# A graph attention layer: steps of 1920 edges at fixed addresses with a carry, in place of one node block per step

## The chip, the core and the metric

The kernel runs on one core of a Trainium2 chip. The metric is the device time of one execution in microseconds (us); lower is better. Five engines work side by side, each through its own instruction stream in order: TensorE (PE; PEld is its weight load), VectorE (DVE), ScalarE (ACT), GpSimd (POOL), and SyncE (SP), which here only issues transfers. They wait for each other on semaphores.

## What is computed

There are 12500 nodes with 64 features, and 212500 edges that are sorted by their target node `dst`. Each edge gets a score, a softmax runs over all edges with the same target, the weighted features of the source nodes are summed, and a dense layer with a residual and a layer norm follows.

```python
h_trans = features @ Watt_w.T + Watt_b
h_src = h_trans[src]
h_dst = h_trans[dst]
e_raw = jnp.sum(h_dst * jnp.tanh(h_src + e_r), axis=-1, keepdims=True)
e_ij = leaky_relu(e_raw * scaling)
max_score = jax.ops.segment_max(e_ij, dst, num_segments=num_nodes)
exp_e = jnp.exp(e_ij - max_score[dst])
denom = jax.ops.segment_sum(exp_e, dst, num_segments=num_nodes)
alpha = exp_e / (denom[dst] + 1e-09)
h_neigh = jax.ops.segment_sum(features[src] * alpha, dst, num_segments=num_nodes)
sum_h = features + h_neigh
prod_h = features * h_neigh
h_out = leaky_relu(sum_h @ W1_w.T + W1_b + (prod_h @ W2_w.T + W2_b))
...
x = _layernorm(x + h_out)
```

## The kernel before

**Head.** TensorE projects all nodes (`project`), VectorE adds the bias and leaves h and x side by side in `hx`; SyncE writes them to `table` in DRAM (L417, L419), one row of 128 numbers for each node. ScalarE and VectorE split all of h into three bf16 parts (`h3`, L629, L1014, L1019). VectorE, TensorE and an indirect transfer find where each block of 128 nodes has its first edge (`find_first`, `set_windows`).

**Steps.** There are 98 blocks of 128 nodes, one a step. A step takes a window of 18 tiles of 128 edges (`MAIN = 17` tiles lie p-major, the `TAIL` tile row by row), starting at the first edge of its block. GpSimd gathers the `table` rows of the sources: one indirect DMA for each tile (L554). The eighteenth tile is gathered only if the block has over 2176 edges; with these inputs the blocks take 1715 gathers. Tiles go in chunks of four (`CHUNK`), so there are five chunks in a step, and three pieces of up to eight tiles.

**The pipeline.** Each engine runs the same function `step(third, before, prev, b, nxt, ahead)`: it works on several blocks at once, b being the newest whose edges are added up, `prev` = b-1, `before` = b-2, `third` = b-3. For b, VectorE adds gathered rows and edge attributes (`add`, L1084), ScalarE takes tanh (L656), TensorE expands h to the edges (`expand`, L819), and VectorE takes the dot products (`dot`, L1095). For `prev` the scores are scanned for their segment maximum: on VectorE across 17 tiles (L1106, L1109), through TensorE into a row (`lay_rows`, L831, L833), two scans along that row (`scan_row`, L1115, L1117), back through TensorE (`lay_back`), and then the exponents' arguments (`exponents`, last line L1128). ScalarE weighs (`weigh`, L681, one activation a tile), TensorE sums (`sum_edges`, L861). For `before` VectorE divides (`neighbours`), TensorE transposes (L867), ScalarE copies (`copy_sum_prod`, L687), TensorE runs the dense layer (`dense`, L872). For `third` VectorE adds the bias, first in its step (L1155), and then the activation, the residual and the moments (`residual`). For `nxt` VectorE builds the one-hot tiles (`place`, `build_hot`, L1073), which TensorE transposes (L805) and ScalarE copies (L651). At a step's end ScalarE prepares the gaps (`set_ids`, L665 to L671) and VectorE writes them (`set_gaps`, L1134, L1135).

**Order and waits.** The order inside a step is that of the calls in each engine's `step`, written by hand. Four steps stand in the body of a hardware loop (`pipeline`: `e.Fori(1, TURNS)`, `BUFS` = 4), so VectorE takes 22 branches back; the first and the last steps are unrolled. GpSimd may gather block b only when the buffer of block b-4 was summed.

**Tail.** The layer norm of all nodes runs after the last step, on GpSimd and VectorE (`normalise`, L369, L371), and SyncE stores four parts of the output (L487, L496).

Of the kernel before, what the change touches and what calls it, by code (L numbers as in the profile page):

```python
# [22 lines left out]
ALU = mybir.AluOpType  # L23
# [7 lines left out]
MAIN = 17  # L31
TAIL = 1
TILES = MAIN + TAIL
# [22 lines left out]
def gnn_layer(nc, x, src, dst, edge_attr, w1, b1, w2, b2, watt, batt, out):  # L56
# [5 lines left out]
    WINDOW = TILES * P  # L62
# [5 lines left out]
    ROW = (2 + TAIL) * P  # L68
    STEPS = [range(a, min(a + STEP, BLOCKS)) for a in range(0, BLOCKS, STEP)]
    ROW_STEP, FIRST_STEP, WINDOW_STEP = 0, 11, 12  # L70
    LAG = 13
    PIECE = STEP * (len(STEPS) // PIECES)
    TURNS = (BLOCKS - 2) // BUFS
# [9 lines left out]
    assert D == 64 and ROWS * SEARCH_ROW == E and TURNS * BUFS + 2 == BLOCKS and BLOCKS % 2 == 0  # L83
    assert (BLOCKS - (PIECES - 1) * PIECE) * D <= MAIN * (2 * D + 1) and BUFS == PIECES
    assert BLOCKS + 1 <= P and ROWS <= P and WINDOW <= E and LAST_NODES > 0

    with ExitStack() as ctx:  # L87
# [13 lines left out]
        def by_piece(name):  # L101
# [11 lines left out]
        h3 = sb("h3", [P, BLOCKS, 3, D], BF16)  # L113
# [17 lines left out]
        bound_i = sb("bound_i", [P, 1], I32)  # L131
        bound = sb("bound", [P, 1])
        bound_row_i = sb("bound_row_i", [P, P], I32)
        bound_row = sb("bound_row", [P, P])
        row_last = sb("row_last", [P, 1])
        below_row = sb("below_row", [P, P])
        row_f = sb("row_f", [P, 1])
        row_idx = sb("row_idx", [P, 1], I32)
        below_n = sb("below_n", [P, 1])
        first = sb("first", [P, 1])  # L140
        first_row = sb("first_row", [1, P + 1])
        next_first = sb("next_first", [P, 1], I32)
        falls = sb("falls", [P, 1])
        row_falls = sb("row_falls", [P, 1])
        over_row = sb("over_row", [1, P])
# [3 lines left out]
        start_row = sb("start_row", [1, P])  # L149
        count_row = sb("count_row", [1, P])  # L150
        start_i = sb("start_i", [1, P], I32)
        count_i = sb("count_i", [1, P], I32)
# [7 lines left out]
        row_i = [sb(f"row_i{k}", [1, ROW], I32) for k in range(2)]  # L160
# [7 lines left out]
        here = sb("here", [P, MAIN])  # L168
        away = sb("away", [P, MAIN])
        gap = sb("gap", [P, MAIN + 1])  # L170
        from_first = sb("from_first", [P, MAIN])
        from_last = sb("from_last", [P, MAIN])
        row_here = sb("row_here", [1, ROW])
        row_gap = sb("row_gap", [1, ROW + 1])
        row_max = sb("row_max", [1, ROW])
        run_max = sb("run_max", [P, MAIN])
        part_max = sb("part_max", [P, MAIN])
        first_max = sb("first_max", [P, MAIN])
        edge_max = sb("edge_max", [P, MAIN])
# [12 lines left out]
        mean_var = sb("mean_var", [P, 2])  # L192

        spare = weight[:, :, :].rearrange("p g n -> p (g n)")
        rows_i = spare[:, 0:SEARCH_ROW].bitcast(I32)
        below = hotT[1][:, :, :].rearrange("p g n -> p (g n)")[:, 0:SEARCH_ROW]
# [3 lines left out]

        hrest = [[hot[2 + j][:, 8 * k:8 * (k + 1), :].rearrange("p g n -> p (g n)").bitcast(F32) for k in range(2)]
                 for j in range(2)]
# [21 lines left out]
        ps_hd = [bank(f"ps_hd{k}") for k in range(3)]  # L224
        ps_hot = [bank(f"ps_hot{k}", BF16) for k in range(2)]
# [3 lines left out]
        ps_sc = [ps_hd[2], ps_row]  # L229
        a_sum = ps_acc[:, 0:D + 1]  # L230
        a_out = ps_acc[:, 256:256 + D]
        row_iota = ps_row[:, ROW:ROW + P // 2].bitcast(BF16)
        numbers = hot[0][:, 0, :]
        m_back = ps_misc[:, 0:2 + TAIL]
        m_spT = ps_misc[:, 128:256]

# [18 lines left out]
        rows_counted = sem("rows_counted")  # L255
        row_ps = sem("row_ps")
        row_ready = sem("row_ready")
        rows_got = sem("rows_got")
        first_ready = sem("first_ready")
        first_ps = sem("first_ps")  # L260
        first_sb = sem("first_sb")
# [5 lines left out]
        part_done = [sem(f"part_done{k}") for k in range(3)]  # L267
# [1045 lines left out]
```

## Time and profile before

| what | value |
|---|---|
| median of 3 runs | 2266.44 us (2265.88 to 2267.22) |
| profiled execution | 2264.81 us, its span 2263.1 us |
| POOL busy | 1655.6 us (73%), x1739 |
| PE busy | 1479.7 us (65%) |
| DVE busy | 1273.0 us (56%) |
| ACT busy | 1085.1 us (48%) |
| granted TensorE clock | 0.5 of 2.4 GHz in the steps |
| moved by DMA | 188.03 MB, 83 GB/s in the mean |

The profiled execution lies 1.6 us under the median. Busy shares are means over the span. A group of instructions is written as line, engine, operation, output<-inputs; after the bar stand the busy time, the mean of one in ns, and the idle time of the engine before them. In the order of time, a row begins with the start and the duration in us, and ends, in brackets, with the idle time of the engine before it and what ended it. "issue" stands for idle time in which the engine waited for nothing that the profile shows.

### The profile page before, as it was taken

What the parts mean: (1) busy time and instruction counts of PE and PEld (TensorE: products, weight loads), DVE (VectorE), ACT (ScalarE), POOL (GpSimd) and SP (SyncE); (2) the same over time, 40 slices, a digit from 0 to 9 for tenths busy, and PEclk for the clock granted to TensorE, in tenths of its full rate; (3) what the DMA queues carried; (4) which work ended last, traced back from release to release, by engine and by line L of the source; (5) the groups of instructions that cost most, each with busy time, mean ns of one, the idle gap of its engine ahead of it and who ended that gap; (6) DMA issues with size and microseconds to landing.
All of it is one profiled execution on the core that took longest, in us unless ns stands there. A gap on an engine that the chain in (4) does not pass through costs nothing.

```text
span 2263.1 us, 43202 instructions
## 1 busy us (share of the span) xinstructions
PE 1479.7 (65%) x11621; PEld 1370.9 (61%) x11621; DVE 1273.0 (56%) x7138; ACT 1085.1 (48%) x3198; POOL 1655.6 (73%) x1739
## 2 busy tenths in 40 slices
PE   3466767667676666676676776766766666766762
PEld 3365656566665666566565665656656665665662
DVE  5556555546556555565555565564655656555554
ACT  3454445545454454545454454544545544454552
POOL 1777777777777777777777777777777777777773
PEclk8555555555555555555555555555555555555555
DMA  8333233232323333232333323333332323323322
GB/s 201 95 76 86 75 86 84 75 85 74 85 75 84 77 83 85 75 85 75 85 82 77 85 74 86 80 79 79 80 86 74 85 77 82 85 74 85 82 67 57
DMA packets 205576, 188.03 MB, mean 83 GB/s; under 512 B 152630, under 2 KB 165228, under 8 KB 205436
## 3 DMA queue, kind: packets, MB, share of 16 engines
q0 software_dynamic: 55040, 113.18, 19.3%
q1 hardware_dynamic: 150396, 73.62, 13.0%
q14 instruction: 129, 1.06, 0.2%
q8 instruction: 11, 0.18, 0.0%
HBM read 177.04 MB, written 9.60 MB: 82 GB/s over the span
## 4 chain that ended last, share of the span: by engine, by line
POOL 64%; issue 24%; POOLq 5%; PE 3%; DVE 1%; DMA 1%; SPq 1%; ACT 1%; DVEq 0%; ACTq 0%
POOL got L554 63%; PE ps_acc L861 2%; POOLq L564 2%; POOLq L544 2%; SPq L417 1%; DMA weight<-in_dst 1%; ACT weight L681 1%; POOL hx L369 0%; DMA got<-table,src_i 0%; POOLq L561 0%; POOLq L87 0%; POOL hx L371 0%; DVE hot L1073 0%; PE ps_hd L758 0%; PE ps_row L769 0%
## 5 line engine op out<-in xcount | busy, mean ns | idle before, releaser
L554 POOL DMA_INDIRECT got<-table,src_i x1715 | 1625.6, 948 | 549.9 <-issue 549.0
L861 PE MATMUL ps_acc<-got,weight 128*128 128x65 f32 x3528 | 805.4, 416 | 253.9 <-ACT weight L681 205.7
L861 PEld LDWEIGHTS ps_acc<-got,weight 128*128 128x128 f32 x3528 | 781.8, 332 | 277.4 <-issue 200.7
L681 ACT ACTIVATE weight<-hot,arg 128x128 f32<-128x128 bf16 x1764 | 544.5, 389 | 44.4 <-DVE arg L1128 44.4
L656 ACT ACTIVATE edge<-edge 128x256 f32<-128x256 f32 (+1 forms) x490 | 190.3, 389 | 761.1 <-DVE edge L1084 749.4
L1095 DVE CUSTOM_DVE_ANT_0 edge<-edge,ps_hd 128x64 f32<-128x64 f32 x1764 | 288.3, 216 | 422.7 <-issue 392.5
L651 ACT ACTIVATE hotT<-ps_hot 128x1024 bf16<-128x1024 bf16 (+1 forms) x294 | 235.8, 803 | 279.9 <-PE ps_hot L805 272.3
L1084 DVE TENSOR_TENSOR edge<-edge,got 128x256 f32<-128x256 f32 (+1 forms) x490 | 196.2, 400 | 249.0 <-DMA got<-table,src_i 240.9
L819 PEld LDWEIGHTS ps_hd<-h,hotT 128*128 128x128 bf16 x5292 | 324.5, 135 | 15.1 <-issue 0.6
L805 PE MATMUL ps_hot<-ident,hot 128*128 128x128 bf16 x1764 | 242.4, 309 | 132.5 <-DVE hot L1073 128.9
L819 PE MATMUL ps_hd<-h,hotT 128*128 (+1 forms) x5292 | 321.1, 242 | 0.4 <-DVE raw L1095 0.4
L805 PEld LDWEIGHTS ps_hot<-ident,hot 128*128 128x128 bf16 x1764 | 185.3, 146 | 166.5 <-DVE hot L1073 162.1
L831 PE MATMUL ps_row<-ident,part_max 128*1 128x128 f32 x196 | 57.4, 396 | 196.0 <-DVE part_max L1109 129.9
L1073 DVE TENSOR_TENSOR hot<-ps_row,dst_rel 128x512 bf16<-128x512 bf16 (+1 forms) x490 | 167.0, 391 | 9.3 <-DVE base L1065 6.7
L1095 DVE DVE_READ_ACCUMULATOR2_ANT raw<- 128x1 f32 x1764 | 144.7, 82 | 2.6 <-issue 2.6
L831 PEld LDWEIGHTS ps_row<-ident,part_max 128*1 128x1 f32 x196 | 10.6, 80 | 209.4 <-issue 209.4
L845 PE MATMUL ps_misc<-ident,row_max 1*128 1x1 f32 x196 | 36.1, 251 | 121.1 <-issue 117.6
L845 PEld LDWEIGHTS ps_misc<-ident,row_max 1*128 1x128 f32 x196 | 30.6, 203 | 134.2 <-issue 134.2
L1117 DVE TENSOR_TENSOR_SCAN row_max<-row_gap,ps_row 1x384 f32<-1x384 f32 x98 | 92.3, 941 | 3.3
L1115 DVE TENSOR_TENSOR_SCAN ps_row<-row_gap,ps_row 1x384 f32<-1x384 f32 x98 | 92.4, 943 | 0.5 <-PE ps_row L833 0.5
L1155 DVE TENSOR_TENSOR z<-ps_acc,b 128x64 f32<-128x64 f32 x98 | 22.0, 225 | 121.2 <-issue 106.7
L872 PE MATMUL ps_acc<-w12T,sum_prodT 128*128 128x64 f32 x196 | 61.8, 419 | 0.4 <-ACT sum_prodT L687 0.4
(120 smaller groups left out, 1059.7 us busy)
## 6 DMA issues: line engine op xcount, KB each, us to landing
edge<-in_edge_attr SPq DMA_DIRECT2D x98, 544.0 KB
got<-table,src_i POOLq DMA_INDIRECT x1715, 2.5
table<-hx SPq DMA_DIRECT2D x12, 512.0 KB
edge<-in_edge_attr SPq DMA_DIRECT2D x98, 32.0 KB
got<-in_x SPq DMA_DIRECT2D x3, 768.0 KB, 14.5
src_i<-in_src SPq DMA_DIRECT2D x98, 8.5 KB
src_i<-in_src SPq DMA_DIRECT2D x98, 0.5 KB
dst_i<-in_dst SPq DMA_DIRECT2D x98, 8.5 KB
```

Of the source, the lines that this page charges most:

```text
L554: pool.indirect_dma_start(got[b.four][:, g, 0:2 * D], None, table, bass.IndirectOffsetOnAxis(ap=src_i[b.four][:, g:g + 1], axis=0))\
L651: act.activation(hotT[b.two][:, a:z, :], ps, ACT.Copy, bias=1.0, scale=-1.0).then_inc(hot_sb[p], 1)
L656: act.activation(edge[b.two][:, a:z, :], edge[b.two][:, a:z, :], ACT.Tanh).then_inc(tanh_done[c], 1)
L681: last = act.activation(weight[:, g, :], hot[b.four][:, g, :], ACT.Exp, bias=arg[:, g:g + 1], scale=-MASKED)
L805: last = pe.transpose(ps_hot[(b.two + p) % 2][:, k * P:(k + 1) * P], hot[b.four][:, g, :], ident16[:, :])
L819: last = pe.matmul(expanded(g), hotT[b.two][:, g, :], rhs, start=(part == 0), stop=(part == 2))
L861: last = pe.matmul(a_sum, weight[:, g, :], got[b.four][:, g, D:2 * D + 1], start=(g == 0), stop=(g == TILES - 1))
L1073: dve.tensor_tensor(hot[b.four][:, a:z, :].rearrange("p g (n a) -> p g n a", a=2), row_iota.rearrange("p (z n a) -> p z n a", z=1, a=2).to ...
L1084: dve.tensor_tensor(edge[b.two][:, a:z, :], edge[b.two][:, a:z, :], got[b.four][:, a:z, 0:D], ALU.add).then_inc(added[c], 1)
L1095: last = dve.tensor_tensor_reduce(out=edge[b.two][:, g, :], in0=edge[b.two][:, g, :], in1=expanded(g), scale=1.0, scalar=0.0, op0=ALU.mult ...
L1115: chain("row", dve.tensor_tensor_scan(ps_row[0:1, 0:ROW], row_gap[:, 0:ROW], ps_row[0:1, 0:ROW], LOWEST, ALU.add, ALU.max), b)
L1117: dve.tensor_tensor_scan(row_max[:, ROW - 1::-1], row_gap[:, ROW:0:-1], ps_row[0:1, ROW - 1::-1], LOWEST, ALU.add, ALU.max).then_inc(row_d ...
```

## The change

A step takes 15 tiles, which are 1920 edges at a fixed address (step n begins at edge 1920 n), whatever nodes they belong to; the last step ends with the last edge. That makes 111 steps (`WINDOWS`) and 1665 gathers. `TAIL` and the conditional gather are gone, and so are the search for first edges and the splitting of h in the head. A step has four chunks and two pieces. The block of 128 nodes of a step begins at the target of its first edge (`base_all`).

A node may have edges in two steps. So the row scan starts from the last value of the step before (`carried`), and the partial sums of the last node go on: `take_carry` on TensorE picks a row of `sums` with `sel`, `copy_carry` on ScalarE brings it to SBUF, and `sum_edges` adds it with `carry_weight`.

What was done for all nodes in the head or the tail is now done in each step: SyncE loads the step's h and x (`load_h`, `load_nodes`), ScalarE and VectorE split h (`split_h`), ScalarE takes a square root (`deviation`), VectorE normalises (`normalise_nodes`), SyncE stores 128 rows (`store_nodes`). VectorE's addition of the dense layer's bias stays first in its step (`add_bias`). `TURNS` becomes 27, with four steps in the loop's body as before.

```diff
-MAIN = 17
-TAIL = 1
-TILES = MAIN + TAIL
+TILES = 15
...
-    TURNS = (BLOCKS - 2) // BUFS
+    TURNS = (FINAL - 2) // BUFS
...
+            def split_h(b, part):
+
+                if part == 0:
+                    act.wait_ge(h_in[b.two], (b.twos + 1) * 16)
+                    if follows(b, 2):
+
+                        act.wait_ge(hd_ready[NP - 1], b.n - 1)
+                    act.activation(h3[b.two][:, 0, :], hw[b.two][:, :], ACT.Copy, scale=SCALE).then_inc(h_high, 1)
+                else:
+                    act.wait_ge(h_left_set, b.n + 1)
+                    act.activation(h3[b.two][:, 1, :], h_left[:, :], ACT.Copy).then_inc(h_mid, 1)
...
+            def deviation(b):
+                act.wait_ge(own["aggr"], b.n + 1)
+                act.activation(std1[:, :], mean_var[:, 1:2], ACT.Sqrt, bias=eps_col[:, 0:1]).then_inc(std_set, 1)
+
+            def copy_carry(b):
+                act.wait_ge(carry_ps, b.n + 1)
+                act.activation(carry_row[:, :], m_carry, ACT.Copy).then_inc(carry_sb, 1)
...
                 if exists(prev):
                     weigh(prev, 1)
+                if exists(before):
+                    copy_sum_prod(before)
+                if exists(prev) and carried(prev):
+                    copy_carry(before)
+                if exists(third):
+                    deviation(third)
                 if exists(b):
                     tanh(b, 3)
-                if exists(before):
-                    copy_sum_prod(before)
-                if exists(prev):
-                    weigh(prev, 2)
-                if exists(nxt):
-                    copy_hot(nxt, 2)
-                if exists(b):
-                    tanh(b, 4)
                     set_ids(b)
...
+            def take_carry(b):
+                pe.wait_ge(own["sum"], b.n + 1)
+                pe.matmul(m_carry, sel[b.four][:, :], sums[:, :], start=True, stop=True).then_inc(carry_ps, 1)
...
+                    if g == TILES - 1 and carried(b):
+
+                        pe.wait_ge(consts, 5)
+                        pe.wait_ge(carry_sb, b.n)
+                        pe.matmul(a_sum[0:1, :], carry_weight[:, :], carry_row[:, :], start=False, stop=False)
...
             def step(third, before, prev, b, nxt, ahead):
                 if exists(third):
-                    residual(third, 0)
+                    add_bias(third)
                 if exists(prev):
                     finish_scores(prev)
                 if exists(third):
-                    residual(third, 1)
+                    finish_nodes(third)
...
                 if exists(prev):
                     exponents(prev)
+                if exists(nxt):
+                    split_h(nxt, 0)
                 if exists(b):
                     add(b, 2)
                     dot(b, 1)
...
                     add(b, 3)
                     dot(b, 2)
-                    add(b, 4)
+                if exists(third):
+                    normalise_nodes(third)
+                if exists(b):
                     dot(b, 3)
-                    dot(b, 4)
                     set_gaps(b)
```

How the instructions stand on ScalarE, in the loop's body, from the second group of weights of a step to the last tanh of the step. Before:

```order
L681 ACTIVATE weight<-hot,arg 128x128 x8
L656 ACTIVATE edge<-edge 128x256
L687 ACTIVATE sum_prodT<-ps_misc 128x128
L681 ACTIVATE weight<-hot,arg 128x128 x2
L651 ACTIVATE hotT<-ps_hot 128x256
L656 ACTIVATE edge<-edge 128x128
L665 ACTIVATE here<-dst_i 128x17
```

The same place of the changed kernel:

```order
L721 ACTIVATE weight<-hot,arg 128x128 x7
L727 ACTIVATE sum_prodT<-ps_misc 128x128
L735 ACTIVATE carry_row<-ps_spare 1x65
L731 ACT_TABLE_LOAD
L731 ACTIVATE std<-mean_var,eps_col 128x1
L691 ACT_TABLE_LOAD
L691 ACTIVATE edge<-edge 128x192
L695 ISA
L700 ACTIVATE here<-dst_i 128x15
```

The tanh of the fourth chunk now stands behind the copies of the products and of the carry and behind a square root with a table load on each side of it; the third group of weights and the third copy of one-hot tiles are gone.

On TensorE, in the loop's body, from the transposes of the one-hot tiles to the dense layer. Before:

```order
L805 MATMUL ps_hot<-ident,hot 128x128 x16
L861 MATMUL ps_acc<-got,weight 128x65 x8
L867 MATMUL ps_misc<-ident,sum_prod 128x128
L861 MATMUL ps_acc<-got,weight 128x65 x8
L805 MATMUL ps_hot<-ident,hot 128x128 x2
L861 MATMUL ps_acc<-got,weight 128x65 x2
L872 MATMUL ps_acc<-w12T,sum_prodT 128x64
```

The same place of the changed kernel:

```order
L842 MATMUL ps_hot<-ident,hot 128x128 x15
L900 MATMUL ps_acc<-got,weight 128x65 x8
L910 MATMUL ps_misc<-ident,sum_prod 128x128
L906 MATMUL ps_spare<-sums,sel 1x65
L900 MATMUL ps_acc<-got,weight 128x65 x6
L899 MATMUL ps_acc<-carry_row,carry_weight 1x65
L900 MATMUL ps_acc<-got,weight 128x65
L915 MATMUL ps_acc<-w12T,sum_prodT 128x64
```

The summing is 15 tiles in two groups where it was 18 in three, and two products for the carry stand among them.

## Rows read from the trace of the kernel before

**Rows 1.** The page: its span, and the group of the gathers.
```profile
span 2263.1 us, 43202 instructions
L554 POOL DMA_INDIRECT got<-table,src_i x1715 | 1625.6, 948 | 549.9 <-issue 549.0
```
**Rows 2.** Busy times by stretch, 300 to 2100 us; then first and last gather (timeline).
```profile
300.00:2100.00 1800.00, 1217.50 (x9580) 1128.24 (x9580) 1020.23 (x5896) 878.33 (x2620) 1362.17 (x1437) 0.50 0.31 81
...
57.22 0.99 POOL L554 DMA_INDIRECT got<-table,src_i  x1 [27.49 <-issue]
...
2204.26 0.94 POOL L554 DMA_INDIRECT got<-table,src_i  x1 [0.30 <-issue]
```
**Rows 3.** Timeline of VectorE over one step of the loop, 1319.95 to 1340.53 us.
```profile
1319.95 0.23 DVE L1155 TENSOR_TENSOR z<-ps_acc,b 128x64 f32<-128x64 f32 x1
...
1327.81 0.17 DVE L1128 TENSOR_TENSOR arg<-score,edge_max 128x17 f32<-128x17 f32 x1
...
1334.44 0.22 DVE L1095 CUSTOM_DVE_ANT_0 edge<-edge,ps_hd 128x64 f32<-128x64 f32 x1 [2.36 <-issue]
...
1338.73 0.22 DVE L1095 CUSTOM_DVE_ANT_0 edge<-edge,ps_hd 128x64 f32<-128x64 f32 x1 [3.64 <-issue]
...
1339.80 0.23 DVE L1134 TENSOR_TENSOR gap<-here 128x16 f32<-128x16 f32 x1 [0.70 <-ACT row_here L671]
...
1340.53 0.23 DVE L1155 TENSOR_TENSOR z<-ps_acc,b 128x64 f32<-128x64 f32 x1
```
**Rows 4.** Timeline of ScalarE and TensorE over the same step.
```profile
1328.02 2.44 ACT L681 ACTIVATE weight<-hot,arg 128x128 f32<-128x128 bf16 x8 [0.35 <-DVE arg L1128]
...
1330.60 3.65 PE L861 MATMUL ps_acc<-got,weight 128*128 128x65 f32 x16 [2.43 <-ACT weight L681]
...
1334.05 0.42 PE L867 MATMUL ps_misc<-ident,sum_prod 128*128 128x128 f32 x1
...
1334.50 0.28 ACT L687 ACTIVATE sum_prodT<-ps_misc 128x128 f32<-128x128 f32 x1 [0.19 <-PE ps_misc L867]
...
1338.30 0.30 ACT L656 ACTIVATE edge<-edge 128x128 f32<-128x128 f32 x1
...
1338.63 0.63 PE L872 MATMUL ps_acc<-w12T,sum_prodT 128*128 128x64 f32 x2
```
**Rows 5.** A turn of four steps by stretch; VectorE where the loop begins anew; waits.
```profile
1386.30:1473.30 87.00, 59.53 (x468) 55.20 (x468) 49.71 (x289) 42.89 (x128) 65.97 (x70) 0.50 0.32 81
...
1299.01 0.23 DVE L1155 TENSOR_TENSOR z<-ps_acc,b 128x64 f32<-128x64 f32 x1 [4.61 <-issue]
...
DVE z L1155 <- issue: 106.7, 22, 5.6
```
**Rows 6.** Timeline of ScalarE around the first square root.
```profile
2208.65 1.28 ACT L693 ACT_TABLE_LOAD   x1
2209.94 0.38 ACT L693 ACTIVATE std<-stats,eps_col 128x93 f32<-128x93 f32 x1
2210.34 1.28 ACT L681 ACT_TABLE_LOAD   x1
```
**Rows 7.** Groups of VectorE's scans and one-hot builds, by form.
```profile
L1117 DVE TENSOR_TENSOR_SCAN row_max<-row_gap,ps_row 1x384 f32<-1x384 f32 x98 | 92.3, 941 | 3.3
...
L1106 DVE TENSOR_TENSOR_SCAN run_max<-gap,score 128x17 f32<-128x17 f32 x98 | 19.2, 196 | 3.3
...
L1073 DVE TENSOR_TENSOR hot<-ps_row,dst_rel 128x512 bf16<-128x512 bf16 x392 | 147.6, 418 | 9.3 <-DVE base L1065 6.7
...
L1073 DVE TENSOR_TENSOR hot<-ps_row,dst_rel 128x256 bf16<-128x256 bf16 x98 | 27.6, 281 | 0.0
```
**Rows 8.** Timeline of VectorE: the bias addition at the first block and in the drain.
```profile
127.55 0.22 DVE L1155 TENSOR_TENSOR z<-ps_acc,b 128x64 f32<-128x64 f32 x1
...
2209.33 0.23 DVE L1155 TENSOR_TENSOR z<-ps_acc,b 128x64 f32<-128x64 f32 x1
...
2225.57 0.23 DVE L1155 TENSOR_TENSOR z<-ps_acc,b 128x64 f32<-128x64 f32 x1 [9.90 <-PE ps_acc L872]
```

More of the change, by code:

```diff
@@ L334, in pipeline, with carried, edge_at @@
                     turn(t, k)
[L335 removed]
+            for k in range(TURNS * BUFS, WINDOWS + 3):
                 turn(0, k)
         def exists(b):
[L339 removed]
+            return not b.known or 0 <= b.n < WINDOWS
+        def carried(b):
+            return not b.known or 0 < b.n < FINAL
+        def edge_at(b):
+            return E - W if b.known and b.n == FINAL else b.n * W
         def follows(b, n):
@@ L411, in _, with load_indices @@
                     .then_inc(bias_in, 16)
+            def load_indices(b):
+                o = edge_at(b)
+                for tile, vector in ((src_i[b.four], src), (dst_i[b.four], dst)):
+                    sp.dma_start(tile[:, :], vector[bass.ds(o, W)].rearrange("(p g) -> p g", g=TILES))\
+                        .then_inc(index_in[b.four], 16)
+            for n in range(2):
+                load_indices(at_block(0, n))
+            sp.wait_ge(old_set, 1)
+            sp.dma_start(out[N - P:N, :], y_old[:, :]).then_inc(stored, 16)
             for s, blocks in enumerate(STEPS):
@@ new lines, in load_nodes, with store_nodes @@
+            def load_nodes(b, n):
+                sp.dma_start(xw[b.four][:, :], x[bass.ds(n, P), :]).then_inc(xw_in[b.four], 16)
+            def store_nodes(b, n):
+                sp.wait_ge(stored, 16 * (b.n + 1))
+                sp.wait_ge(y_done, b.n + 1)
+                sp.dma_start(out[bass.ds(n, P), :], y_out[b.two][:, :]).then_inc(stored, 16)
+                if b.known and b.n == FINAL - 1:
+                    sp.wait_ge(stored, 16 * (FINAL + 1))
+                    sp.dma_start(y_old[:, :], out[N - P:N, :]).then_inc(old_in, 16)
@@ L679, in weigh @@
                     act.wait_ge(summed[p], b.n)
+                if p == 0 and carried(b):
+                    if follows(b, 2):
+                        act.wait_ge(summed[NP - 1], b.n)
+                    act.activation(carry_weight[:, :], carry_arg[:, :], ACT.Exp)
                 for g in range(*piece(p)):
@@ L844, in lay_back @@
                 for k in range(2):
-                    pe.transpose(m_back[:, k:k + 1], row_max[0:1, k:2 * P:2], ident[0:1, 0:1])
-                for k in range(TAIL):
-                    last = pe.transpose(m_back[:, 2 + k:3 + k], row_max[0:1, (2 + k) * P:(3 + k) * P], ident[0:1, 0:1])
+                    last = pe.transpose(m_back[:, k:k + 1], row_max[b.two][0:1, k:ROW:2], ident[0:1, 0:1])
                 last.then_inc(back_ps, 1)
@@ L1206, in step @@
                 if exists(before):
-                    neighbours(before)
+                    dve.wait_ge(xw_in[before.four], (before.fours + 1) * 16)
+                    neighbours(before, xw[before.four][:, :])
+                if exists(nxt):
+                    split_h(nxt, 1)
                 if exists(b):
```

589 lines of the change are left out of this document (294 added, 295 removed).

## The prediction

> **What bounds the kernel now.** I read the page first, then busy times by stretch, then the steps in the order of time. By the page GpSimd looks like the bound: 1715 gathers, each 948 ns busy with some 0.3 us of issue around it [rows 1]. Between 300 and 2100 us it makes 1437 gathers, one in 1.2526 us, and never pauses between the first at 57.2 and the last at 2204.3 us [rows 2]. A block with 17 or 18 gathers (17.5 in the mean) thus takes 21.9 us, four take 87.7 us. If that were all, 1665 gathers in place of 1715 would save 63 us, and the work taken out of the tail some 30 more.
>
> The timeline of a single step says otherwise. From one bias addition to the next VectorE takes 20.58 us [rows 3], and in this step it waits for no gather; its waits are 2.36 and 3.64 us before dot products (for tanh on ScalarE) and 0.70 us for the gaps. A whole turn of the loop without such a wait takes 87.0 us [rows 5], against 87.7 us for its gathers. So two chains run at nearly the same pace: the gathers, and a circle through VectorE, ScalarE and TensorE. The change lightens the first one. What matters is the second, and it has to be read link by link.
>
> **The circle before.** Count from A, the start of the last argument instruction at 1327.81. From the bias addition to A are 7.86 us of VectorE [rows 3]. From A: ScalarE starts the weights at A+0.21 and TensorE the sums at A+2.79; the transpose of the products follows 3.45 us later (eight tiles), ScalarE copies it at A+6.69; the summing of the rest, the third group of one-hot tiles and the last tanh follow, at A+10.49; VectorE's next bias addition comes 2.23 us after that tanh, at A+12.72 [rows 3, 4].
>
> **The circle after, first half.** The two scans along the row shrink from 384 to 256 elements. The slope from 17 to 384 elements is (941-196)/367 = 2.0 ns, so each saves 0.26 us, together 0.52 [rows 7]. The last two one-hot builds of a step, 512 and 256 wide (418 and 281 ns), become one of 384, about 350 ns: 0.35 less, or 0.27 as such instructions overlap by some 0.08. The copy of the moments goes (0.1 on the path); the carry's argument takes the place of the tail's, and the base is a copy from a table: +0.05. 7.86-0.52-0.27-0.10+0.05 = 7.02 us.
>
> **Second half.** ScalarE has an exponential of one element for the carry before the weights: +0.10 (nearest rows say 0.1 to 0.3). The sums start at A+2.89, the transpose at A+6.34, its copy at A+6.79. TensorE runs at its lower clock of 1.2 GHz, 0.50 granted, throughout [rows 5], and I keep that. The carry's product takes two TensorE passes of 0.22 us each (3.45 us for sixteen) behind the transpose, so ScalarE copies the carry at A+7.15 and is done at A+7.4. Now comes the square root. Exp and tanh share a table in the steps before, where no load is seen; the square root is the one function that brings loads. From the start of one load to the start of the next are 1.69 us with a square root of 93 columns [rows 6], 1.61 with one column; with the second load of 1.28 these are 2.9 us, in every step, ahead of the tanh of the last chunk. This tanh starts at A+10.3, at the same place as before, though three tiles of work are gone. From it to the next bias addition are 2.23 us, +0.05 for 192 instead of 128 columns, -0.25 for shorter row instructions: A+12.34. The splitting of h, `normalise_nodes` and the shorter weights lie in waits: VectorE's 2.36 and 3.64 us before dot products shrink but don't vanish. If that cover were gone, they would cost their 0.2 us each, some 1 us.
>
> So a straight step takes 7.02+12.34 = 19.36 us, 1.22 us less than before, with three tiles less. Fifteen gathers take 18.8 us. The gathers are no longer the bound; GpSimd will wait for free buffers.
>
> **A rule against the trace.** Around the first square root the load begins 0.02 us behind the instruction before it, and the square root 0.01 us after the load's end [rows 6]. The Trainium skill, ScalarE: Activation LUTs, What ACT_TABLE_LOAD costs, gives 1283 ns for the load, as here, and about 1380 ns of drain on top. The trace here shows no such drain. By that figure a step would be longer by 2.8 us and the kernel, as an estimate, by some 300 us. I go by the rows and keep the rule as a rival. The same page says to batch functions of one set; the change does the reverse of that, which fits the 2.9 us above.
>
> **Branches back.** Where the loop begins anew, VectorE sits idle 4.61 us before its bias addition although TensorE has long delivered; there are 22 such waits, 106.7 us in all, as many as branches back [rows 5]. The body still has four steps, so I keep this: a turn of 87.0 us becomes 87.0 - 4 x 1.22 = 82.1 us. There are 26 turns now, for 104 steps.
>
> **The sum.** The first bias addition for a real block came at 127.55 us [rows 8], 52 gathers and 5.2 us after the first gather at 57.2 [rows 2]. The head loses the search but gains six small transfers ahead of the table's, so I leave the first gather at 57 us; with 45 gathers the addition comes at 119 us. Then 108 steps to the drain: 26 x 82.1 + 4 x 19.4 - 4.7 (the last turn has no branch back; 87.0 - 4 x 20.58 = 4.7) = 2207 us, so the drain starts at 2326 us, where before it started at 2209.3 us. The drain's first step took 16.2 us [rows 8] and becomes 15; the last two blocks, a square root each, and a store, a read of the stored rows and a last store one behind the other, about 15 more. The layer norm and the large stores of the tail are gone. 2326+30 = 2356 us of span. With 1.7 us around it, as in the profiled execution of before, that is 2358 us, against 2264.8 us: 4.1% slower. As that execution lies 1.6 us under the median, the comparison with the median is the same within 0.1%.
>
> In short: from the first bias addition to the drain, 95 steps in 2082 us become 108 steps in 2207 us, +125 us; the first addition comes 8.5 us earlier, and from the drain's start to the end there are 30 us in place of 53.8, which gives back 24.
>
> **Bounds.** Each 0.1 us in a step is 11 us. The unknown small instructions (exponential and copies of the carry, three more on ScalarE's queue, waits with registers) leave a step between 18.9 and 19.9 us: 2308 to 2416 us. A branch back of nothing to 7 us: -118 to +55 us. Head and drain: 10 us either way.
>
> **Rivals.** *TensorE's half becomes the last link.* The bias addition waits for `dense`, which stands behind the sums with their two carry products. I get its end at A+11.3, 1 us before VectorE asks. Should the carry cost TensorE over 1 us more, VectorE waits at the start of each step; 0.5 us beyond that point costs 54 us: about 2412 us. For it: two waits between engines stand in the middle of the sums. Against it: TensorE's share falls from 18 to 15 tiles. 0.13.
>
> *The drain exists.* 2.8 us a step, 300 us: about 2660 us. 0.03, as the rows show none.
>
> *The square root is off the path (faster).* If tanh came early enough in spite of it, TensorE's half would decide, A+11.3: 1.0 us a step less, 2250 us, 0.7% faster. It decides as soon as under 1.9 us of the 2.9 are left on the path. Against it: the instruction order leaves ScalarE no choice. 0.05.
>
> *The branch back gets cheap (faster).* Without these 4.7 us the time would be 2358 - 25 x 4.7 = 2240 us, 1.1% faster; the sign turns where under 1 us of them is left. Against it: all 22 branches of before show it, and the body is only some 7% shorter. 0.07.
>
> *The gathers stay the bound (faster).* Both chains shorter than I think: 57+1665 x 1.2526 = 2143, +36 for the last chunk and the drain = 2180 us, 3.8% faster. It needs steps of 18.8 us with the branch in them, 1.7 us less than I count. 0.04.
>
> **The numbers.** The forecast, 2358 us, has 0.68. Its own range is 2300 to 2420. For 8 in 10 I take 2290 to 2435 us: the three faster cases (0.16) stay outside, TensorE's is inside. A measurement tells 0.2% from no change. Faster by over 0.2% are these three, 0.16; within 0.2% I leave 0.02, taken from the forecast's low end; slower is the rest, 0.82.
>
> **What would show it.** In the trace of the changed kernel: two table loads a step, 2.9 us between the carry's copy and the tanh of three tiles; VectorE idle before the dot products of the last chunk; straight steps of 19.4 us and turns of 82 us; GpSimd waiting for the sums of TensorE (before, 0.9 us in all [rows 1]), over 5% of the span; the drain after 2320 us. Wrong it is if VectorE waits for gathers in most steps, if its wait for ScalarE's last tanh is absent, or if it waits for `dense` in every step and not once a turn.

## The result: 2.4% faster, where 4.1% slower was forecast

The changed kernel takes 2212.27 us (median of 4, 2211.41 to 2212.53), the kernel before 2266.58 us (median of 4, 2265.88 to 2267.22). The ratio is 0.9759, with a 95% interval of 0.9747 to 0.9770. The forecast was 2358 us, its range began at 2290. The profiled execution took 2212.15 us, with a span of 2210.4 us, so the sum of the prediction (a span of 2356 us) is 146 us too high.

### The profile page after: what moved, and what is told of

Same layout as the page of the kernel before. It is cut to its first block, busy times and chain, and to the rows that moved or that the text cites. A ratio compares the mean times of both kernels' runs of the same rounds, so it can differ in the third digit from the quotient of the medians.

```text
span 2210.4 us, 44930 instructions
## 1 busy us (share of the span) xinstructions
PE 1523.2 (69%) x11357; PEld 1326.2 (60%) x11357; DVE 1259.5 (57%) x7377; ACT 1401.7 (63%) x3892; POOL 1594.2 (72%) x1678
## 4 chain that ended last, share of the span: by engine, by line
ACT 32%; DVE 30%; PE 21%; issue 11%; POOL 2%; SPq 2%; DVEq 1%; DMA 0%; ACTq 0%; POOLq 0%
PE ps_acc L900 18%; ACT weight L721 11%; ACT L691 6%; ACT L731 6%; DVE hot L1097 5%; DVE edge L1108 4%; DVE ps_row L1140 3%; DVE edge L1119 3%; POOL got L595 2%; DVE row_gap L1163 2%; ACT edge L691 2%; PE ps_spare L906 2%; ACT row_here L706 2%; ACT std L731 1%; DVE edge_max L1150 1%
## 5 line engine op out<-in xcount | busy, mean ns | idle before, releaser
L595 POOL DMA_INDIRECT got<-table,src_i x1665 | 1587.2, 953 | 539.9 <-issue 506.9
L900 PEld LDWEIGHTS ps_acc<-got,weight 128*128 128x128 f32 x3330 | 735.4, 329 | 359.5 <-issue 342.9
L721 ACT ACTIVATE weight<-hot,arg 128x128 f32<-128x128 bf16 x1665 | 506.3, 384 | 5.3 <-DVE arg L1156 5.3
L1119 DVE CUSTOM_DVE_ANT_0 edge<-edge,ps_hd 128x64 f32<-128x64 f32 x1665 | 267.6, 213 | 124.7 <-ACT edge L691 122.8
L857 PE MATMUL ps_hd<-h,hotT 128*128 128x64 bf16 x4995 | 311.1, 242 | 10.5 <-DVE h L1088 10.5
L842 PE MATMUL ps_hot<-ident,hot 128*128 128x128 bf16 x1665 | 213.1, 306 | 148.9 <-DVE hot L1097 148.9
L1203 DVE RECIPROCAL rstd<-std 128x1 f32<-128x1 f32 x111 | 18.2, 164 | 497.4 <-ACT std L731 497.4
L842 PEld LDWEIGHTS ps_hot<-ident,hot 128*128 128x128 bf16 x1665 | 155.8, 138 | 186.2 <-DVE hot L1097 186.2
L674 ACT ACTIVATE hotT<-ps_hot 128x1024 bf16<-128x1024 bf16 x222 | 212.3, 956 | 19.0 <-PE ps_hot L842 17.7
L691 ACT ACT_TABLE_LOAD x108 | 138.6, 1283 | 1.9
L727 ACT ACTIVATE sum_prodT<-ps_misc 128x128 f32<-128x128 f32 x111 | 30.8, 277 | 85.0 <-PE ps_misc L910 85.0
L1140 DVE TENSOR_TENSOR_SCAN ps_row<-row_gap,row_max,ps_row 1x256 f32<-1x256 f32 x109 | 80.2, 736 | 0.0
```

Of the source, the lines that this page charges most:

```text
L595: pool.indirect_dma_start(got[b.four][:, g, 0:2 * D], None, table, bass.IndirectOffsetOnAxis(ap=src_i[b.four][:, g:g + 1], axis=0))\
L674: act.activation(hotT[b.two][:, a:z, :], ps, ACT.Copy, bias=1.0, scale=-1.0).then_inc(hot_sb[p], 1)
L691: act.activation(edge[b.two][:, a:z, :], edge[b.two][:, a:z, :], ACT.Tanh).then_inc(tanh_done[c], 1)
L721: last = act.activation(weight[:, g, :], hot[b.four][:, g, :], ACT.Exp, bias=arg[:, g:g + 1], scale=-MASKED)
L842: last = pe.transpose(ps_hot[p][:, k * P:(k + 1) * P], hot[b.four][:, g, :], ident16[:, :])
L857: last = pe.matmul(expanded(g), hotT[b.two][:, g, :], h3[b.two][:, part, :], start=(part == 0), stop=(part == 2))
```

## The profile after, beside that of before

The page of the changed kernel: its span, the gathers, the queue that brings instructions, and the chain that ended last (share of the span by engine).

```profile
span 2210.4 us, 44930 instructions
...
q14 instruction: 18, 0.15, 0.0%
...
ACT 32%; DVE 30%; PE 21%; issue 11%; POOL 2%; SPq 2%; DVEq 1%; DMA 0%; ACTq 0%; POOLq 0%
...
L595 POOL DMA_INDIRECT got<-table,src_i x1665 | 1587.2, 953 | 539.9 <-issue 506.9
```

The chain no longer runs through GpSimd: it is ScalarE, VectorE and TensorE that hand each other the work. So the gathers ceased to be the bound, as forecast. The page of before has this row for the same queue of instructions:

```profile
q14 instruction: 129, 1.06, 0.2%
```

That is 111 packets of instructions more than after. The prediction does not use this row.

One straight step on VectorE, ScalarE and TensorE (timeline: start, duration, engine and line, idle time before in brackets). It answers to [rows 3, 4]. It is the shortest of its turn: by position behind the branch, the four steps take 19.40, 19.29, 18.92 and 19.07 us in the mean of 25 turns.

```profile
1000.38 0.23 DVE L1186 TENSOR_TENSOR z<-ps_acc,b 128x64 f32<-128x64 f32 x1
...
1003.96 0.24 DVE L1071 TENSOR_SCALAR dst_rel<-dst_i,base 128x30 bf16<-128x30 int32 x1
...
1007.08 0.16 DVE L1156 TENSOR_TENSOR arg<-score,edge_max 128x15 f32<-128x15 f32 x1
...
1009.95 3.65 PE L900 MATMUL ps_acc<-got,weight 128*128 128x65 f32 x16 [2.48 <-ACT weight L721]
...
1014.16 0.22 ACT L735 ACTIVATE carry_row<-ps_spare 1x65 f32<-1x65 f32 x1
1014.39 1.28 ACT L731 ACT_TABLE_LOAD   x1
1015.68 0.29 ACT L731 ACTIVATE std<-mean_var,eps_col 128x1 f32<-128x1 f32 x1
1016.00 1.28 ACT L691 ACT_TABLE_LOAD   x1
...
1017.29 0.36 ACT L691 ACTIVATE edge<-edge 128x192 f32<-128x192 f32 x1
...
1017.59 0.63 PE L915 MATMUL ps_acc<-w12T,sum_prodT 128*128 128x64 f32 x2
...
1019.27 0.23 DVE L1186 TENSOR_TENSOR z<-ps_acc,b 128x64 f32<-128x64 f32 x1
```

Counted from A, the start of the argument instruction at 1007.08: the first half took 6.70 us (forecast 7.02), the carry's copy stands at A+7.08 (7.15), the last tanh at A+10.21 (10.3), TensorE's dense ends at A+11.1 (11.3), the second half took 12.19 us (12.34). Between the carry's copy and the last tanh stand the two table loads with the square root.

VectorE's waits over the whole span (total, times, longest):

```profile
DVE rstd L1203 <- ACT std L731: 497.4, 111, 7.2
...
DVE edge L1119 <- ACT edge L691: 122.8, 108, 1.3
...
DVE z L1186 <- DVE row_gap L1163: 13.1, 27, 0.5
```

VectorE waits 4.5 us a step for the square root (497.4 / 111) and 1.1 us for the last tanh. At the branch back there are 0.5 us in all, where before there were 4.85 us in the mean (106.7 / 22) [rows 5]. A turn of four steps took 76.65 us; 82.1 were forecast:

```profile
1000.38:1077.03 76.65, 54.32 (x408) 47.18 (x406) 44.73 (x264) 50.48 (x140) 58.07 (x61) 0.50 0.32 84
```

The first bias addition and those of the drain:

```profile
117.74 0.23 DVE L1186 TENSOR_TENSOR z<-ps_acc,b 128x64 f32<-128x64 f32 x1 [2.12 <-PE ps_acc L915]
...
2186.17 0.23 DVE L1186 TENSOR_TENSOR z<-ps_acc,b 128x64 f32<-128x64 f32 x1
2200.33 0.23 DVE L1186 TENSOR_TENSOR z<-ps_acc,b 128x64 f32<-128x64 f32 x1 [0.88 <-PE ps_acc L915]
2204.57 0.23 DVE L1186 TENSOR_TENSOR z<-ps_acc,b 128x64 f32<-128x64 f32 x1
```

So the 146 us are: the first addition 1.3 us earlier than forecast; 108 steps in 2068.4 us (2186.17 - 117.74) in place of 2207, 138.6 us; the drain 24.2 us in place of 30, 5.8 us. The step with the branch back takes 0.3 us more than the others (19.40 beside 19.09 us in the mean), where 4.7 were forecast. So of the 138.6 us, 25 x 4.4 = 110 are the branches back; the other 29 are 0.27 us a step.

## Experiments

The question is why the stall at the branch back is gone, and what it would have cost. Theory A: it is a matter of place. VectorE's instructions are fetched in packets, few are held (kept in the engine), and whether the loop's body is still held at the branch depends on where its ends lie between the edges of the packets. Theory B: of size, the body being short enough now. Theory C: the stall had another cause, outside VectorE's stream.

In the built programs, counted with waits and register instructions, VectorE's loop body has 356 instructions at 557 to 913 before, and 341 at 491 to 832 after. (The first expectations count without waits.)

To move the body and nothing else, K tiny instructions are put ahead of the loop, inside a wait of 15.5 us that VectorE has there for its first rows:

```
             dve.memset(ones[:, :], 1.0)
+            for k in range(K):
+                dve.memset(filler[:, k:k + 1], 1.0)
```

### First set: 70, 140, and 60 in the kernel before

> The changed kernel with 70 tiny instructions more on VectorE (one column each, into a tile that nobody reads) ahead of the first step, inside a wait of 16 us for the first rows. Nothing in the loop changes; only the place of the loop's body in VectorE's instruction stream does, from about 424 to 713 (counted without waits) to about 494 to 783. Theory A (place): the branch back costs its 4 to 5 us when the body of VectorE's loop lies over two multiples of 256 instructions (before: 472 to 787, over 512 and 768) and nothing when it lies over one (after: 424 to 713, over 512 alone). It expects 25 waits of about 4.7 us ahead of the bias addition, 2212 + 25 x 4.7 = about 2330 us, and about as many packets in the queue of instructions as before had (129, against 18 of after). Theory B (size): the body is short enough at 289 instructions and was too long at 315, wherever it lies: 2212 us and 18 packets, no change. Theory C (other engines, or the gathers): what vanished was never VectorE's own; 2212 us, no change. The Trainium skill, Runtime: NRT & Kernel Launch, Instruction fetch mechanics, says that instructions come in blocks of 256, that an engine holds two of them, and that a taken branch out of these two has to fetch its target first; theory A is this rule applied to VectorE.

> The changed kernel with 140 such instructions ahead of the first step: the loop's body stands at about 564 to 853, over 768 alone. Theory A (place) expects no wait at the branch back and 2212 us within 0.3%, although the stream is longer than in the run with 70. If any growth of the stream brought the stall back, it would be here as well, about 2330 us. Theories B and C: 2212 us.

> The kernel before with 60 such instructions ahead of the first step: its loop's body of 315 instructions moves from about 472 to 787 to about 532 to 847, over 768 alone. Theory A (place): the 22 waits of 4.6 to 4.9 us go, and the packets of the instruction queue fall from 129 to under 30; the time hardly moves (2255 to 2267 us, 0 to 0.5% less), since the gathers, at 1.2526 us each and never pausing, set 87.7 us for a turn whose circle took 87.0 with the stall. What VectorE no longer waits for at the branch it then waits for at gathered rows. Theory B (size): the stall stays in place, 2266 us, 129 packets. If the gathers did not set the pace of before, the time would fall by the stall, 22 x 4.7 = 103 us, to about 2165 us.

The chip of these runs took 3864 us for the kernel before, so of this set only places and counts of packets are used. The packets of instructions were 143 with 70, 144 with 140, and 129 in the kernel before with 60. (The times were 3224, 3210 and 3859 us.) The first fits theory A and speaks against B and C: the same body of 341 instructions is fetched anew in every turn. The second and the third contradict theory A as I had put it, with blocks of 256.

The records of the single packets gave the right sizes. Each carries 8192 bytes. In a turn of before there are five: two behind the branch back, and three when VectorE has started about 586, 718 and 841 instructions of its program; in the run with 140 the places are about 719, 836 and 971. So an edge comes about every 128 instructions, at about the same places of the program in both. That one is fetched ahead and four are held is inferred: a body that touches three packets would stay held, one that touches four would lose its first. Then 70 (561 to 902), 140 (631 to 972) and 60 in before (617 to 973) all touch four.

### Second set: 20, 110, 43 in the kernel before

> The changed kernel with 20 tiny instructions more on VectorE ahead of the first step. The records of the earlier runs give theory A (place) its right numbers: the instructions of VectorE come in packets of 8 KB, one each 128 instructions; in before five packets come in every turn of the loop, two of them behind the branch back, the others when VectorE is about 586, 714 and 842 instructions into its program (counted with waits and registers), so edges lie at 74 + 128 k. Four packets are held, and one more is fetched ahead, so a body that touches three packets stays held and one that touches four has to be fetched anew at each branch back. Body of before: 557 to 913, four packets (edges 586, 714, 842). Of after: 491 to 832, three (586, 714). With 20 more it is 511 to 852, over the edge at 842 too: four. Theory A expects the wait at the branch back to return (25 x 4.3 to 5 us): 2320 to 2335 us, and 135 to 150 packets in the queue of instructions. Theory B (size alone, 341 instructions against 356) expects 2212 us and 18 packets. The runs with 70 and 140 had over 140 packets, which speaks against B already, but not in a time that can be set beside the 2212 us.

> The changed kernel with 110 such instructions: the body lies at 601 to 942, over the edges at 714 and 842 alone: three packets. Theory A (place): no wait at the branch back, under 25 packets in the queue of instructions, 2212 us within 0.3%. A theory by which every lengthening of the head brings the stall back, in the way that the runs with 70 and 140 did: 2325 us and over 130 packets.

> The kernel before with 43 such instructions: its body of 356 moves from 557 to 913 to 600 to 956, over the edges at 714 and 842 alone: three packets. Theory A: the 22 waits of 4.6 to 4.9 us ahead of the bias addition go, and so do over 100 packets of instructions. The time hardly moves, as the gathers (1.2526 us each, 87.7 us a turn) pace this kernel: 2252 to 2267 us, 0 to 0.6% less. Theory B (the longer body is too long wherever it lies): 129 packets, 2266 us, the waits where they were. If the circle and not the gathers had set the pace of before: 22 x 4.7 = 103 us less, 2163 us.

Measured, on a chip with before at 2270.57 us:

| run | body | time, us | ratio to before | packets |
|---|---|---|---|---|
| 20 more | 511 to 852 | 2275.87 | 1.0023 (1.0013 to 1.0032) | 143 |
| 110 more | 601 to 942 | 2212.51 | 0.9746 (0.9729 to 0.9762) | 19 |
| before, 43 more | 600 to 956 | 2269.01 | 0.9994 (0.9985 to 1.0004) | 19 |

The bodies of 110 and 43 have the same row of packets on their pages:

```profile
q14 instruction: 19, 0.16, 0.0%
```

With 20, the queue of instructions on the page, and VectorE's waits ahead of the bias addition:

```profile
q14 instruction: 143, 1.17, 0.2%
```
```profile
DVE z L1189 <- issue: 77.8, 25, 3.4
```

The same waits with 110:

```profile
DVE z L1189 <- DVE row_gap L1166: 13.4, 27, 0.6
```

In the kernel before with 43, these and the waits for gathered rows:

```profile
DVE edge L1087 <- DMA got<-table,src_i: 620.9, 404, 4.1
...
DVE z L1158 <- DVE row_gap L1138: 11.5, 23, 0.6
```

And the waits for gathered rows in the kernel before as it was:

```profile
DVE edge L1084 <- DMA got<-table,src_i: 240.9, 164, 3.9
```

Theory A holds in both kernels and both ways. 20 instructions bring the stall to the changed kernel, 110 do not; 43 take it from the kernel before, although its body is no shorter. Size alone (B) and another cause (C) are out. In the kernel before the time did not follow: what VectorE no longer waited at the branch it waited for gathered rows, 620.9 us in place of 240.9. The circle with its stall was hidden by the gathers there.

One number missed: with 20 I expected 2320 to 2335 us. The stall is back in all 25 places but costs 63 us (2275.87 - 2212.51), 2.5 us each: it is 3.1 us long here (77.8 / 25, with the usual 0.5 us in it), 4.85 in before (106.7 / 22, [rows 5]).

### Where the edge lies

> The changed kernel with 8 tiny instructions more on VectorE ahead of the first step: the loop's body lies at 499 to 840, its end just short of the edge at 842. Theory A (place, edges at 74 + 128 k) expects no wait at the branch back, under 25 packets in the queue of instructions and 2212 us within 0.2%; 12 instructions more, as in the run with 20, gave 143 packets and 2276 us. If the edge lies lower than I read it, or if the few instructions between the last step and the branch count twice, the stall is here already: 2276 us and over 140 packets.

2278.98 us beside 2274.14 of before, ratio 1.0021 (1.0012 to 1.0031), 143 packets. VectorE's waits ahead of the bias addition:

```profile
DVE z L1189 <- issue: 80.3, 25, 3.5
```

My reading of the edge was too high by a few instructions. A likely reason is that the count goes by instructions that had started, and the fetch runs ahead of them. A body that ends at 832 is held, one that ends at 840 is not, so the edge lies between, and the others 128 apart. All nine bodies agree with this. The changed kernel escapes the stall by at most 8 instructions; 8 more in front of it cost 2.7% (1.0021 beside 0.9759). Neither the shorter body nor its earlier start would have done alone, by this rule: 341 instructions from 557 end at 898, 356 from 491 end at 847, both over the edge. That sum wasn't run.

The Trainium skill, Runtime: NRT & Kernel Launch, Instruction fetch mechanics, says that a taken branch out of the pages held forces a fetch of its target before execution goes on; the traces agree (a fetch in every turn, and VectorE idle until it has come). It gives blocks of 256 instructions and two of them held. By that a body would stall where it has two edges inside, 256 apart. The stalls at 557 to 913 and at 511 to 852 then need an edge between 557 and 596, and the stall at 631 to 972 needs one between 631 and 716: no place of the edges gives both. The traces show packets of 128, and the measurement decides.

### Why the stall was longer in the kernel before

From VectorE's branch in the records, in us: the start of the packet with the branch's target, the first packet of the bulk load of edge features (544 KB before, 480 KB after), and the bias addition.

| kernel | target packet | bulk load | bias addition |
|---|---|---|---|
| before | 2.0 to 3.3 | 0.3 to 0.9 | 4.2 to 5.5 |
| changed, 20 more | 1.0 to 1.3 | 1.9 to 2.0 | 2.9 to 3.2 |
| before, bulk load later | 1.0 to 1.3 | 2.5 to 2.9 | 2.9 to 3.3 |

Busy times by stretch in the kernel before around one such branch (at 1030.2; the bias addition follows at 1034.98). The last three columns are TensorE's clock, the busy share of the DMA engines and GB/s.

```profile
1031.00:1032.00 1.00, 0.00 (x0) 0.00 (x0) 0.00 (x0) 0.00 (x0) 0.70 (x2) 0.50 0.49 164
1032.00:1033.00 1.00, 0.00 (x0) 0.00 (x0) 0.00 (x0) 0.00 (x0) 0.69 (x2) 0.50 1.03 418
1033.00:1034.00 1.00, 0.00 (x0) 0.00 (x0) 0.00 (x0) 0.00 (x0) 0.72 (x1) 0.50 0.82 173
```

The packets of instructions and the bulk load both go through the DMA engines, and for a microsecond these are busy throughout, while VectorE, TensorE and ScalarE stand still. The experiment issues the bulk load some 2 us later, in the kernel before:

```
-                sp.dma_start(edge[b.two][:, 0:MAIN, :], ...)
-                sp.dma_start(edge[b.two][:, MAIN:TILES, :], ...)
+                for q in range(0, P, P // 4):
+                    sp.dma_start(edge[b.two][q:q + P // 4, MAIN:TILES, :], ...)
+                sp.dma_start(edge[b.two][:, 0:MAIN, :], ...)
```

> The kernel before, stall and all, with one thing changed on SyncE: the small load of the last tile's edge features (32 KB) goes ahead of the large one (544 KB), and in four pieces, so that the large load is issued some 2 us later. It is about the size of the stall: 4.6 us in before, where the first packet of the large load starts 0.35 to 0.75 us behind VectorE's branch and the packet of instructions that the branch asks for only 2.0 to 3.2 us behind it; 2.9 us in the run with 20, where the large load starts 1.9 us behind the branch and the instructions come at 1.0 us. If the instructions queue behind the large load in the DMA engines, they come at 1.0 us here too, and the waits ahead of the bias addition at the branch fall from 4.2 to 5.5 us to 2.9 to 3.2 us. If the difference is of another kind (the longer body, the place of the target), the waits stay over 4.2 us. The time stays near 2268 us in either case (the gathers pace this kernel), or rises if the edges come too late.

The same waits here:

```profile
DVE z L1156 <- issue: 70.0, 22, 3.4
```

All 22 waits fell, from 4.85 us in the mean to 3.18 (70.0 / 22). So the bulk load had held the instructions up, most likely as they queued behind it. The time was 2278.19 us, ratio 1.0017 (1.0007 to 1.0026): again the gathers hid what was saved, and VectorE waited 429.2 us for gathered rows in place of 240.9.

### The square root off the path

On ScalarE, the square root is moved from ahead of the last tanh to behind the first:

```
                 if exists(b):
                     tanh(b, 0)
+                if exists(third):
+                    deviation(third)
+                if exists(b):
                     tanh(b, 1)
...
-                if exists(third):
-                    deviation(third)
                 if exists(b):
                     tanh(b, 3)
```

> The changed kernel with the square root (and so its two table loads, 2.9 us with it) taken from between the tanh of the third chunk and the tanh of the last one to between the first and the second tanh of the step, where VectorE has delivered its variance as well. If the loads on the path set the step (19.07 to 19.4 us straight, as forecast), the last tanh comes up to 2.9 us earlier, and TensorE's dense end at A+11.1 us (11.1 + 6.7 = 17.8 us, with the bias addition behind it about 18.2) or the gathers (15 x 1.2526 = 18.8 us) become the bound: 104 to 108 steps at 18.8 us in place of 19.16 us, 2170 to 2185 us. If the loads delay the middle tanhs by as much as they save, no change: 2212 us. If they delay the middle ones and VectorE falls behind there by more, up to 2.9 us a step in the worst case: 2300 us and more.

It took 3112.92 us on the chip of the first set, ratio 0.8056; beside the changed kernel's 2212 us this says nothing. So it was run again with the second set.

> The changed kernel with the square root and its two table loads between the first and the second tanh of a step, in place of ahead of the last one; VectorE's instructions and their place are those of after. If the 2.9 us of the loads on the way to the last tanh set the step (18.9 to 19.4 us), TensorE's dense end (A+11.1 us, a step of about 18.2 us) or the gathers (15 x 1.2526 = 18.8 us a step) come last instead: 2170 to 2185 us. If the loads cost as much at the new place as at the old, 2212 us. If they hold up the middle chunks by more, up to 2300 us.

2169.78 us, ratio to before 0.9559 (0.9543 to 0.9575), on the chip where the changed kernel with 110 more took 2212.51 us: 1.9% less. It is the fastest version. In the step that ends in the lines below (1000.54 to 1019.29 us) TensorE was at its lower clock, 0.50 granted, as in the changed kernel, so the step is not short by a faster clock; over 300 to 2100 us the granted clock was 0.55, beside 0.51 in the changed kernel. The chain and the gathers on its page, then its timeline:

```profile
POOL 71%; issue 24%; PE 1%; DMA 1%; POOLq 1%; DVE 1%; SPq 1%; ACT 0%; DVEq 0%
...
L595 POOL DMA_INDIRECT got<-table,src_i x1665 | 1575.7, 946 | 532.6 <-issue 507.2
```
```profile
1003.38 1.28 ACT L731 ACT_TABLE_LOAD   x1
...
1006.28 0.42 ACT L691 ACTIVATE edge<-edge 128x256 f32<-128x256 f32 x1
...
1019.29 0.22 DVE L1187 TENSOR_TENSOR z<-ps_acc,b 128x64 f32<-128x64 f32 x1 [2.12 <-PE ps_acc L916]
```

The chain runs through GpSimd again, and VectorE waits 2.1 us a step for TensorE's dense, as the rival on the square root had it; but both stand behind the gathers, 15 x 1.25 us a step. The same kernel with the stall brought back, and the changed kernel without a square root:

> The changed kernel with the early square root and with 20 tiny instructions more ahead of the first step, so that the branch back stalls again (over 140 packets of instructions, some 2.6 us each, as in the run with 20 alone, where it cost 63 us). With the early square root GpSimd's gathers set the pace (15 x 1.25 = 18.75 us a step, GpSimd never pausing) and VectorE waits 2 to 3.5 us a step for gathered rows and 2.1 us for TensorE. Theory: a stall of VectorE costs time only where its circle paces the kernel; here it is taken out of those waits, and the time stays at 2170 us within 0.4%. Rival: the stall stands in the circle with TensorE as well (bias addition behind dense), which is at nearly the same pace, and costs its 25 x 2.6 = 65 us: 2233 us.

> The changed kernel with Identity in place of the square root of the variance (the square root is left out; all else is done), so that no table is loaded in the loop. It prices the loads at their old place: 2.9 us off ScalarE ahead of the last tanh. Behind it comes TensorE's dense end, or the gathers at 15 x 1.25 us = 18.75 us a step: about 2168 us, the same as with the early square root, if the loads are fully hidden there; 2160 or less if they still cost something at their new place.

They took 2182.5 us (0.9595, 0.9579 to 0.9611) and 2187.65 us (0.9611, 0.9595 to 0.9627), on a chip with before at 2274.14 us: 0.6% and 0.9% over the 2170 and 2168 us that I expected. The rows of the gathers, with the early root and 20 more, then without a square root:

```profile
L596 POOL DMA_INDIRECT got<-table,src_i x1665 | 1587.3, 953 | 531.4 <-issue 507.3
```
```profile
L595 POOL DMA_INDIRECT got<-table,src_i x1665 | 1594.7, 958 | 532.6 <-issue 507.0
```

Against the early square root alone, the gathers were busy 11.6 and 19.0 us longer, and the spans are 10.9 and 19.8 us longer (2179.0 and 2187.9 beside 2168.1 us). The idle time before the gathers is the same (531.4 and 532.6 beside 532.6 us). So both differences are those of the gathers themselves, which took 953 and 958 ns in the mean in place of 946. Why is open: it is not the chip alone, as the mean went from 946 to 954 ns between kernels on the chip of the second set too. The stall is there in all 25 turns (21 of the waits, 66.4 us, stand under issue) and made GpSimd pause no longer, where it had cost 63 us in the changed kernel. And leaving the square root out gives nothing over moving it: its loads are hidden at the new place.

## Why the prediction was wrong, step by step

**Branches back: the step that failed.** "The body still has four steps, so I keep this" put 25 x 4.7 = 118 us into the sum. The runs showed 0.3 us for each, so 110 of the 146 us are this step. The rival with the right outcome (2240 us, 2212 measured) was there, at 0.07; the other 28 us are shorter steps and a shorter drain. Against it I held that all 22 branches of before show the stall and that the body is only some 7% shorter. That is a repetition of the symptom, no cause. I kept a stall whose cause I had not found, through a change that altered what it hangs on. The page of before had the trace of it: 129 packets of instructions, some five for each branch. With the branch back missed, the changed kernel takes 2276 us, 0.2% slower than before: the sign of the result hung on where the body lies.

**The size of the term.** Even where the stall comes back, it costs 2.5 us over a branch without it (with 20 more, the step with the branch takes 22.0 us in place of 19.4), not 4.7. The difference to before is the bulk load in front of the fetch, and that collision belonged to the old timing of SyncE against VectorE.

**First half: 0.2 us too long.** 7.02 us were forecast; the step shown has 6.70, the mean of all turns is 6.83. The scans (0.73 and 0.67 us) came as forecast. Missing in the sum was the row of the relative addresses (dst_rel). In the two steps that are compared it went from 0.46 to 0.24 us, and with the base the pair went from 0.68 to 0.43 us from start to start. But the step of [rows 3] was slow in this row. The first line below is that step's; the others are the means over all steps, before and after:

```profile
1324.08 0.46 DVE L1062 TENSOR_SCALAR dst_rel<-dst_i,base 128x36 bf16<-128x36 int32 x1
...
L1062 DVE TENSOR_SCALAR dst_rel<-dst_i,base 128x36 bf16<-128x36 int32 x98 | 27.2, 278 | 1.6 <-issue 1.6
...
L1071 DVE TENSOR_SCALAR dst_rel<-dst_i,base 128x30 bf16<-128x30 int32 x111 | 27.0, 244 | 3.9
```

By the means this row gives 0.03 us a step. A sum that starts from one step inherits what was unusual in it; where the rest of the 0.2 us lies is open.

**Second half: right.** 12.34 against 12.19 us, each link within 0.2 us. The two loads cost 2.9 us ahead of the last tanh (1014.39 to 1017.29), and no drain stands behind or ahead of them: the square root begins 0.01 us behind the load's end. The rival with the drain is out.

**TensorE's half** ended at A+11.1 and VectorE waited for dense only at the start and in the drain. That rival was rightly put aside, and so was the one that gathers stay the bound, though by little: 18.8 us against a step of 19.2.

**GpSimd's waits: wrong.** I wanted to see over 5% of the span in waits for TensorE. They are 6.7 us in all, 0.3% of the span. GpSimd's idle time is 539.9 us for 1665 gathers, nearly all of it the usual 0.3 us of issue. With turns of 76.65 us and not 82 it had little to wait for.

**Head and drain** gave 7 us less than forecast, inside their bounds.

**The square root off the path** was costed at 1.0 us a step at most (TensorE deciding); it gave 43 us, 0.4 us a step, as the gathers decide first.

## What to carry to other kernels

A stall at a loop's branch is to be traced to its cause before it is kept in a forecast: compare the packets of the instruction queue with the number of turns, and count the loop's body against the 128-instruction edges, its place as well as its length. By the rule found here a body of under 384 instructions can be moved into three packets with some filler ahead of it, at no cost where the head waits anyway; the runs show it for 341 and 356. Such a stall, like a table load, costs time only on the chain that paces the kernel: where another one does, as the gathers here, taking it away gives nothing.

## What was not expected of the hardware

- VectorE's instructions come in packets of 8192 bytes, one each 128 instructions. A loop over three of them ran without a fetch, 0.4 us from the branch to the next instruction that works; over four it fetched five packets a turn, and these were 3.0 us in the mean where the fetch started ahead of the bulk load and 4.7 us behind one of 544 KB.
- TensorE's body of 449 instructions in the kernel before spans more than three such packets, yet all five packets of a turn stand at places of VectorE's program. TensorE evidently holds more. The Trainium skill, Runtime: NRT & Kernel Launch, Instruction fetch mechanics, gives it four times the store of the others; how much it is, no run here shows.
- One indirect gather of 128 rows took 946 to 960 ns in the mean from run to run, on one chip too (946 to 954), and in a kernel that they pace the step from 946 to 958 alone made 0.9% of the time. The cause is open.
- On one chip every kernel ran much longer, before at 3864 us, with gathers as elsewhere (946 to 960 ns) and long idle times between engines. The cause is open.
